# A routed expert layer behind a scan: three more tiles fixed early, twelve row places, and one weight copy on another engine

## The chip, the cores and the metric

The kernel runs on one core of a Trainium2 chip. The metric is device time in microseconds, the median of the runs shown. The trace is of one profiled execution. Its engines are TensorE (PE; PEld are its weight loads), VectorE (DVE), ScalarE (ACT), GpSimd (POOL) and SyncE (SP), each with its own instruction stream that runs in order; they meet in semaphores.

## The reference, cut to what matters

```python
x = L0_attn_x                                   # [2, 2048, 128]
mod = (_silu(c) @ wmod).reshape(2, 6, 1, -1)    # sa, ca, ga, sb, cb, gb
h = _layernorm(x) * (1 + ca) + sa
x = x + ga * linear_scan_block(h)               # gates by block-diagonal products, then a scan over the tokens
h = _layernorm(x) * (1 + cb) + sb
logits = _silu(h @ rw1 + rb1) @ rw2 + rb2       # 128 -> 512 -> 8
k_prob, k_index = softmax(top_2(logits))
for e in range(8):                              # out = sum over the two chosen experts
    we = sum(where(k_index == e, k_prob, 0))
    out += we * (_silu(h @ w1[e] + b1[e]) @ w2[e] + b2[e])   # 128 -> 512 -> 128
x = x + gb * out
```

## The kernel before, in words

The 4096 tokens are eight groups of 512. For every group the kernel normalizes (`stats1`, `norm1`), turns the rows (`turn_x`), makes the gates (`gates`, on ScalarE `tanh`, `decay`), scans, adds the residual, normalizes again and runs the router (`router`, `logits`, `sum`). VectorE chooses two experts for each token (`top2`), TensorE counts the ranks (`rank`), and `place` works out each row's place in a buffer in HBM that is sorted by expert. GpSimd sends the rows there: `send:0` to `send:15`, four indirect transfers each, 64 in all, eight for a group (L556).

The expert part works on 39 whole tiles of 256 sorted rows with one expert each. For tile s: SyncE loads the rows (L421) and TensorE transposes them (`tx`, L1234). VectorE copies them out (`xT`, L1010) and copies the expert's first and second weights (`w1`, L1019, and `w2`, L1028) after it has read the expert's number from a table into a register. TensorE runs layer 1 (`l1`, L1245), ScalarE applies silu (`hid`, L665), TensorE runs layer 2 (`l2`, L1263), ScalarE adds the bias (`yb`, L674), TensorE transposes back (`ty`, L1273), VectorE scales (`sc`, L1036), and GpSimd scatters the rows to their tokens (`scat`, two transfers of 1.0 us, L567). The transposes `tx` and `ty` share one PSUM bank, so each waits until VectorE has read the one before it.

Which tile is which expert stands in a table `tab`. `table1` (VectorE, L946 to L956) fixes the first nine tiles (`EARLY`) from the counts of the first four groups. `table1b`, `table1c` (L970 to L980) and `table2`, `table3` work out the other 30 from counts after four, six, seven and eight groups. SyncE loads tiles 0 to 8 once the sends of groups 0 to 3 have landed. The sends of groups 4 to 7 count on one semaphore, `s_disp[1]`; tiles 9 and 10 are loaded when all of it has come, and tile 10 also waits for the scatter of tile 0, because there are ten row places (`U`) in SBUF. At step 31 the hardware loop has ended, and the steps 31 to 36 also sum two expert outputs of a group into the result (`combine`, L1055 to L1057, on VectorE); step 40 and what follows sum the last groups.

The order up to tile 10 or so is written out by hand in `PLAN`, a list of steps for each engine. On VectorE the part around the tables reads

```python
norm2:7 place:4 table1:0 w1:0 top2:5 place:5 xT:0 xT:1 w2:0 table1b:0+top2:6 place:6 w1:1 table1c:0
w1:2 xT:2 xT:3 w1:3 w2:1 rowsB:0 sc:0 w2:2 top2:7 ...
```

and on TensorE

```python
... l1:0 router:31 rank:6 lev:0 tx:2 l2:0 l1:1 logits:7 tx:3 l1:2 ty:0 sum:7 l2:1 tx:4 l1:3 rank:7 ...
```

At the start TensorE's list is `warm:0 turnc:0 warm:1 mod:0 warm:2 turn_x:0 gates:0 turnb:0 turn_x:1`. `warm` are products that nobody reads. `turnb` transposes the biases (L1102) and waits for their three loads, which ScalarE orders at the start.

Of the kernel before, what the change touches and what calls it, by code (L numbers as in the profile page):

```python
# [14 lines left out]
P = 128  # L15
# [4 lines left out]
def adaln_block(nc, x, a_param, w_in, w_a, rw1, rb1, rw2, rb2, w1, b1, w2, b2, c, wmod, out):  # L20
# [25 lines left out]
    FIRST = 11  # L46
# [9 lines left out]
    LATE = TILES - EARLY  # L56
# [8 lines left out]
    with ExitStack() as ctx:  # L65
# [65 lines left out]
        yo = shared[:, 0:U * SL].rearrange("p (u n d) -> p u n d", u=U, d=D)  # L131
# [51 lines left out]
        xr = tx[:, 0:U * HALVES * ROW].rearrange("p (u n r) -> p u n r", u=U, n=HALVES)  # L183
# [29 lines left out]
        s_xnp = sem("s_xnp")  # L213
        s_root = sem("s_root")
# [16 lines left out]
        s_sc = sems(*(f"s_sc{i}" for i in range(U)))  # L231
# [22 lines left out]
        def tiles(g):  # L254
# [6 lines left out]
                warm:0 turnc:0 warm:1 mod:0 warm:2 turn_x:0 gates:0 turnb:0 turn_x:1 gates:1 turn_x:2 warm:3 turn_x:3  # L261
# [10 lines left out]
                tx:11 l1:10 ty:8 l2:9""",  # L272
# [6 lines left out]
                norm2:7 place:4 table1:0 w1:0 top2:5 place:5 xT:0 xT:1 w2:0 table1b:0+top2:6 place:6 w1:1 table1c:0  # L279
                w1:2 xT:2 xT:3 w1:3 w2:1 rowsB:0 sc:0 w2:2 top2:7 xT:4 w1:4 place:7 w2:3 sc:1 w1:5 xT:5 w2:4 table2:0  # L280
                sc:2 w1:6 xT:6 sc:3 xT:7 w2:5 w1:7 w2:6 sc:4 w2:7 xT:8 table3:0 sc:5 w1:8 w1:9 sc:6 w2:8 xT:9 w2:9
                w1:10 xT:10 sc:7 xT:11 w1:11 sc:8 w2:10""",
# [8 lines left out]
                share:5 silu:29 lgc:6 silu:30 hid:0 share:6 silu:31 hid:1 lgc:7 yb:0 hid:2 yb:1 share:7 hid:3 yb:2  # L291
                hid:4 yb:3 hid:5 yb:4 hid:6 yb:5 hid:7 yb:6 hid:8 yb:7 hid:9 yb:8 hid:10""",
# [44 lines left out]
        def levels_of(name):  # L337
            return turn_bank(name, 0)[:, 0:2 * NE]
# [25 lines left out]
        def expert_steps(eng, body, last):  # L364
            with eng.Fori(0, ROUNDS) as n:
                for u in range(U):
                    body(n * U + FIRST + u, (FIRST + u) % U)
            for s in range(FIRST + ROUNDS * U, last):
                body(s, s % U)
# [7 lines left out]
        def rounds(s, u):  # L377

            return (s - u) // U + 1

        def landed(eng, last):
            for u in range(U):
                eng.wait_ge(s_sc[u], 16 * HALVES * ((last - u) // U + 1))
# [9 lines left out]
        def _(sp):  # L393
# [22 lines left out]
            def load(s, u):  # L416
                r = sp.value_load(tab[0:1, 0, bass.ds(s, 1)], min_val=0, max_val=NE * REG)
                if not (static(s) and s < U):

                    sp.wait_ge(s_sc[u], 16 * HALVES * (rounds(s, u) - 1))  # L420
# [14 lines left out]
            for s in range(EARLY):  # L435
                if s * HALVES * ROW + HALVES * ROW > GPB * G and s * HALVES * ROW <= GPB * G:
                    sp.wait_ge(s_y, NG)
                load(s, s % U)
# [4 lines left out]
            sp.wait_ge(s_tab, 2)  # L443
            sp.wait_ge(s_pad, 16 * (NE + 1))
            sp.wait_ge(s_disp[1], 16 * TOPK * GPB * GT)
            for s in range(EARLY, FIRST):
                load(s, s % U)
# [34 lines left out]
        def _(pool):  # L482
# [67 lines left out]
            def dispatch(n):  # L550
# [27 lines left out]
        def _(act):  # L578
# [90 lines left out]

            def bias_out(s, u):  # L670
                act.wait_ge(s_l2, s + 1)
                if not (static(s) and s < 2):
# [6 lines left out]
                           "share": second_share, "hid": lambda s: hidden(s, s % U),  # L679
                           "yb": lambda s: bias_out(s, s % U)})  # L680
# [8 lines left out]
            def step(s, u):  # L689
                if static(s) and s >= TILES - 1:  # L690
                    if s == TILES - 1:
                        bias_out(s - 2, (u - 2) % U)
                        bias_out(s - 1, (u - 1) % U)
                        hidden(s, u)
                        bias_last(s, u)
                    return
                if not static(s) or s < TILES + 2:
                    bias_out(s - 2, (u - 2) % U)
                if not static(s) or s < TILES:
                    hidden(s, u)  # L700

# [6 lines left out]
        def _(dve):  # L708
# [168 lines left out]
            def place(g):  # L877
# [5 lines left out]
                dve.wait_ge(s_pos, g + 1)  # L883
                place_of = rank_bank(g).rearrange("p (j e) -> p j e", e=NE)
# [26 lines left out]
            def constants(_):  # L911
# [5 lines left out]
                v.tensor_copy(w2_s[:, :].rearrange("p (e w) -> p e w", e=NE)[:, :, HC * D:W2E], b2_c)  # L917
# [14 lines left out]
                v.memset(base[:, NENT:NENT + 1], float(4 * NE * REG))  # L932
                yield from link(v.memset(val2[:, 1, :], 1.0))
# [25 lines left out]
            def entries(_):  # L959
# [6 lines left out]
                yield from link(v.tensor_tensor(row_0[:, 0:1], row_p[:, 0:1], base[:, 0:1], ALU.add))  # L966

            def middle_levels(_):
                dve.wait_ge(s_lev, 1)
                v.tensor_tensor(cmpl[:, :, :, :], levels_of("lev").rearrange("p (l e) -> p l e", l=2).unsqueeze(3)  # L970
                                .to_broadcast([P, 2, NE, KT]),
                                kthr[:, :, 0, :].unsqueeze(1).to_broadcast([P, 2, NE, KT]), ALU.is_gt).then_inc(s_levr, 1)
                dve.wait_ge(s_levr, 1)
                yield from link(v.tensor_reduce(reach[:, :, :], cmpl[:, :, :, :], AX.X, ALU.add))
                v.tensor_tensor(nent[:, NE:2 * NE], reach[:, 0, :], full[:, :, 0], ALU.subtract)
                v.tensor_tensor(nent[:, 2 * NE:3 * NE], reach[:, 1, :], reach[:, 0, :], ALU.subtract)
                yield from link(v.scalar_tensor_tensor(base[:, 2 * NE:NENT].rearrange("p (l e) -> p l e", l=2), reach[:, :, :],
                                            float(SL), ereg[:, :].unsqueeze(1).to_broadcast([P, 2, NE]),
                                            ALU.mult, ALU.add))
                yield from link(v.tensor_tensor(dbase[:, :], base[:, 1:NENT + 1], base[:, 0:NENT], ALU.subtract))  # L980

            def late_table(_):
# [5 lines left out]
                yield from link(v.tensor_tensor(nent[:, 3 * NE:NENT], nent[:, 3 * NE:NENT], reach[:, 1, :], ALU.subtract))  # L988
# [347 lines left out]
```

## Time and profile before

| | us |
|---|---|
| median of 3 runs | 289.26 |
| lowest, highest | 288.16, 289.66 |
| the profiled execution | 288.93 |
| its span in the trace | 287.2 |
| TensorE busy | 254.2 (89%) |
| VectorE busy | 188.9 (66%) |
| GpSimd busy | 170.0 (59%) |
| ScalarE busy | 166.9 (58%) |

The profiled execution takes 1.7 us more than its span, for what lies around it. A busy share is a mean over stages with different limits; the stages have to be read one by one. The waits tell what came last at each place.

### The profile page before, as it was taken

How to read it: one execution, taken by the hardware profiler on the slowest of the kernel's cores; microseconds unless marked ns; L12 is line 12 of the kernel's file. 1: busy time of each engine (PE TensorE's matmuls, PEld its weight loads, DVE VectorE, ACT ScalarE, POOL GpSimd, SP SyncE). 2: the span in 40 equal slices, each digit the busy share in tenths (PEclk: the TensorE clock that was granted, in tenths of full speed). 3: DMA queues.
4: the chain of work that ended last, by engine and by line, in shares of the span. 5: the costliest groups of instructions: out<-in, count | busy, mean ns of one | idle time of the engine just before them, and what ended most of it. 6: DMA issues, size and time to landing. Idle time of an engine off the chain costs nothing.

```text
span 287.2 us, 4973 instructions
## 1 busy us (share of the span) xinstructions
PE 254.2 (89%) x1187; PEld 177.0 (62%) x1187; DVE 188.9 (66%) x751; ACT 166.9 (58%) x323; POOL 170.0 (59%) x192
## 2 busy tenths in 40 slices
PE   7886997998889997999998999999999999989910
PEld 3343443354244334787877888888888888867800
DVE  3959999999999987576443444444444446868333
ACT  4169999999885445544554555555555555444400
POOL 3994311267777757777777777545554545635650
PEclk9999999999999999999999999999999999999975
DMA  7994010121131226413423433222216822290504
GB/s 212 306 333 126 19 38 26 51 66 59 46 119 54 88 74 154 126 48 111 141 71 107 110 102 110 53 76 75 65 55 194 237 74 74 75 265 4 160 0 146
DMA packets 45365, 30.51 MB, mean 106 GB/s; under 512 B 5085, under 2 KB 41999, under 8 KB 45342
## 3 DMA queue, kind: packets, MB, share of 16 engines
q1 hardware_dynamic: 39888, 21.49, 27.5%
q0 software_dynamic: 4544, 8.47, 8.9%
q10 hardware_dynamic: 910, 0.30, 0.4%
q8 instruction: 8, 0.13, 0.2%
q14 instruction: 15, 0.12, 0.1%
HBM read 16.39 MB, written 12.67 MB: 101 GB/s over the span
## 4 chain that ended last, share of the span: by engine, by line
PE 43%; POOL 23%; issue 14%; DVE 12%; DMA 5%; DVEq 1%; ACT 1%; POOLq 0%; ACTq 0%; SPq 0%
POOL sorted_rows L556 21%; PE bank L1263 18%; PE bank L1245 17%; PE bank L1273 3%; PE bank L1234 2%; DVE st L722 2%; DMA expert_out<-shared,tx 2%; PE bank L1150 1%; POOL shared L520 1%; PE bank L1151 1%; PE bank L1090 1%; DVE tx L816 1%; DVE hT L821 1%; DVE shared L742 1%; DMA xs<-in_L_attn_x_dram 1%
## 5 line engine op out<-in xcount | busy, mean ns | idle before, releaser
L567 POOL DMA_INDIRECT expert_out<-shared,tx x78 | 79.3, 1016 | 54.1 <-DVE shared L1036 37.6
L665 ACT ACTIVATE hT<-bank,w_t 128x256 f32<-128x256 f32 x156 | 65.5, 471 | 29.5 <-PE bank L1245 28.6
L556 POOL DMA_INDIRECT sorted_rows<-rows,sloti x64 | 64.1, 1001 | 27.2 <-issue 18.3
L1263 PE MATMUL bank<-hT,w_t 128*128 128x256 f32 x312 | 74.1, 380 | 0.0
L1245 PE MATMUL bank<-xT,w_t 128*128 128x256 f32 x312 | 74.0, 380 | 0.0
L1245 PEld LDWEIGHTS bank<-xT,w_t 128*128 128x128 f32 x312 | 56.3, 190 | 6.6 <-DVE w_t L1019 0.5
L1263 PEld LDWEIGHTS bank<-hT,w_t 128*128 128x128 f32 x312 | 56.2, 190 | 6.3
L674 ACT ACTIVATE yT<-bank,w_t 128x256 f32<-128x256 f32 x38 | 18.0, 474 | 46.3 <-PE bank L1263 46.3
L1174 PE MATMUL bank<-h2T,rw_s 128*128 128x512 f32 x64 | 33.5, 623 | 1.0 <-ACT qv L652 0.5
L1010 DVE COPY xT<-bank 128x256 f32<-128x256 f32 x39 | 16.4, 422 | 22.4 <-PE bank L1234 22.4
L1036 DVE TENSOR_TENSOR shared<-bank,tx 128x256 f32<-128x256 f32 x38 | 16.1, 424 | 19.7 <-PE bank L1273 19.6
L1028 DVE COPY w_t<-w_s 128x513 f32 x39 | 17.8, 457 | 16.5 <-issue 15.6
L1019 DVE COPY w_t<-w_s 128x516 f32 x39 | 17.3, 443 | 16.1 <-issue 14.9
L1114 PE MATMUL bank<-ident 128*128 128x512 f32 x30 | 17.7, 702 | 2.0 <-POOL ident L492 2.0
L722 DVE BATCH_NORM_STATS2 st<-xs 128x6 f32<-128x128 f32 x64 | 15.7, 282 | 4.5 <-DMA xs<-in_L_attn_x_dram 4.4
L1174 PEld LDWEIGHTS bank<-h2T,rw_s 128*128 128x128 f32 x64 | 10.0, 189 | 12.6 <-issue 5.9
L1234 PE MATMUL bank<-ident,tx 128*128 128x128 f32 x78 | 15.2, 276 | 2.1 <-DMA tx<-sorted_rows 1.4
L1273 PE MATMUL bank<-ident,yT 128*128 128x128 f32 x76 | 14.7, 275 | 1.9 <-DVE xT L1010 1.5
L1234 PEld LDWEIGHTS bank<-ident,tx 128*128 128x128 f32 x78 | 10.4, 141 | 8.0 <-issue 2.5
L1273 PEld LDWEIGHTS bank<-ident,yT 128*128 128x128 f32 x76 | 10.1, 141 | 7.4 <-issue 4.2
L652 ACT ACTIVATE qv<-bank,smallbT 128x512 f32<-128x512 f32 x16 | 10.8, 686 | 6.4 <-PE bank L1174 6.4
L512 POOL TENSOR_TENSOR rs<-ve,half_neg 128x4 f32<-128x4 f32 x8 | 8.6, 1087 | 9.4 <-DVE ve L729 9.4
(198 smaller groups left out, 326.6 us busy)
## 6 DMA issues: line engine op xcount, KB each, us to landing
tx<-sorted_rows SPq DMA_DIRECT2D x39, 130.0 KB, 2.3
w_s<-in_L_ffn_w_dram SPq DMA_DIRECT2D x16, 256.0 KB, 6.0
xs<-in_L_attn_x_dram SPq DMA_DIRECT2D x8, 256.0 KB, 5.3
rows<-rows SPq DMA_DIRECT2D x8, 256.0 KB, 2.6
av<-expert_out SPq DMA_DIRECT2D x8, 256.0 KB, 3.7
qv<-expert_out SPq DMA_DIRECT2D x6, 256.0 KB, 5.3
expert_out<-shared,tx POOLq DMA_INDIRECT x78, 2.4
sorted_rows<-padr SPq DMA_DIRECT2D x9, 130.0 KB, 2.8
```

The source lines that it names most:

```text
L556: p.indirect_dma_start(sorted_rows[:, :], bass.IndirectOffsetOnAxis(ap=sloti[:, k, t:t + 1], axis=0), rows[:, t, k, :], None).then_inc(s_d ...
L567: p.indirect_dma_start(expert_out[:, :], bass.IndirectOffsetOnAxis(ap=xr_i[:, s % U, n, D + 1:D + 2], axis=0), yo[:, s % U, n, :], None, b ...
L665: ins = nc.scalar.activation(hsT[:, u % 2, h, :], bank[4 + q][:, (h % 2) * SL:(h % 2 + 1) * SL], ACT.Silu, bias=w1_t[:, u % 2, HID + h:HID ...
L674: nc.scalar.activation(yT[:, u % 2, :], out_bank(s)[:, 0:SL], ACT.Identity, bias=w2_t[:, u % 2, HC * D:W2E]).then_inc(s_yT_e, 1)
L722: ins = v.bn_stats(st[:, t, :], xs[:, t, :])
L1028: v.tensor_copy(w2_t[:, u % 2, :], w2_s[:, bass.ds(e * W2E, W2E)]).then_inc(s_w2t, 1)
L1114: t.matmul(bank[to][:, :].rearrange("p (k q) -> p k q", q=P), ident[:, :], ident[:, :].unsqueeze(1).to_broadcast([P, 512 // P, P]), start= ...
L1174: t.matmul(bank[2 + n % 2][:, :], rw1_s[:, h * P:(h + 1) * P], h2T[:, g % 2, :], start=True, stop=True).then_inc(s_rl1, 1)
L1234: ins = t.transpose(bank[1][:, n * P:(n + 1) * P], xr[:, u, n, 0:D], ident[:, :])
L1245: ins = t.matmul(bank[4 + h // 2][:, (h % 2) * SL:(h % 2 + 1) * SL], w1_t[:, u % 2, h * P:(h + 1) * P], xT[:, u % 2, :], start=True, stop= ...
L1263: ins = t.matmul(out_bank(s)[:, 0:SL], w2_t[:, u % 2, h * D:(h + 1) * D], hsT[:, u % 2, h, :], start=(h == 0), stop=(h == HC - 1))
L1273: ins = t.transpose(bank[1][:, n * P:(n + 1) * P], yT[:, u % 2, n * P:(n + 1) * P], ident[:, :])
```

## The change

`FIRST` goes from 11 to 12: the loops start at tile 12. A second step of the table, `tablem`, fixes tiles 9 to 11 from the counts after six groups (a product added to `rank:6`, copied out in `place:6`), `tablen` takes them off the rest, and `table1c` becomes smaller. The sends of groups 4 and 5 get their own semaphore; behind it SyncE loads tiles 9 to 11, ahead of the pads. There are twelve row places; the two new ones hold tiles 0 and 1, the other tiles go round in ten as before. The second weights are copied by ScalarE (`weights2`, right behind `hid` in the loop, ahead of it in most of the written order), no longer by VectorE. TensorE's `turnb:0` stands ahead of `warm:1`. The sums move to steps 32 to 36 and 38.

```diff
-    FIRST = 11
+    FIRST = 12
+    SLOTS = 12
+    NEXT = FIRST - EARLY
...
-                warm:0 turnc:0 warm:1 mod:0 warm:2 turn_x:0 gates:0 turnb:0 turn_x:1 gates:1 turn_x:2 warm:3 turn_x:3
+                warm:0 turnc:0 turnb:0 warm:1 mod:0 warm:2 turn_x:0 gates:0 turn_x:1 gates:1 turn_x:2 warm:3 turn_x:3
...
-                norm2:7 place:4 table1:0 w1:0 top2:5 place:5 xT:0 xT:1 w2:0 table1b:0+top2:6 place:6 w1:1 table1c:0
-                w1:2 xT:2 xT:3 w1:3 w2:1 rowsB:0 sc:0 w2:2 top2:7 xT:4 w1:4 place:7 w2:3 sc:1 w1:5 xT:5 w2:4 table2:0
+                norm2:7 place:4 table1:0 w1:0 top2:5 place:5 xT:0 xT:1 table1b:0+top2:6 place:6 w1:1 tablem:0 tablen:0
+                table1c:0 w1:2 xT:2 xT:3 w1:3 rowsB:0 sc:0 top2:7 xT:4 w1:4 place:7 sc:1 w1:5 xT:5 table2:0 sc:2 w1:6
...
-                share:5 silu:29 lgc:6 silu:30 hid:0 share:6 silu:31 hid:1 lgc:7 yb:0 hid:2 yb:1 share:7 hid:3 yb:2
+                share:5 silu:29 lgc:6 silu:30 hid:0 w2:0 share:6 silu:31 hid:1 w2:1 lgc:7 yb:0 w2:2 hid:2 yb:1 w2:3
+                share:7 hid:3 yb:2 w2:4 hid:4 yb:3 w2:5 hid:5 yb:4 w2:6 hid:6 yb:5 w2:7 hid:7 yb:6 w2:8 hid:8 yb:7
...
-        SUMS = {FIRST + ROUNDS * U: 0, FIRST + ROUNDS * U + 1: 1, FIRST + ROUNDS * U + 2: 2,
-                FIRST + ROUNDS * U + 3: 3, MID + 12: 4, FIVE + 5: 5, TILES + 1: 6}
+                FIRST + ROUNDS * U + 3: 3, FIRST + ROUNDS * U + 4: 4, TILES - 1: 5, TILES + 1: 6}
+        def slot(s):
+            return U + s if s < SLOTS - U else s % U
...
+            sp.wait_ge(s_tab, 2)
+            sp.wait_ge(s_disp[1], 16 * TOPK * GPB // 2 * GT)
+            for s in range(EARLY, FIRST):
+                load(s, slot(s))
             sp.wait_ge(s_pads, 1)
...
-                            rows[:, t, k, :], None).then_inc(s_disp[t // (GPB * GT)], 16)
+                            rows[:, t, k, :], None).then_inc(s_disp[max(0, t // GT - GPB + 2) // 2], 16)
...
+            def weights2(s, u):
+                if static(s) and s == 0:
+                    act.wait_ge(s_tab, 1)
+                if static(s) and s == EARLY:
+                    act.wait_ge(s_tab, 2)
+                e = act.value_load(tab[0:1, 1, bass.ds(s, 1)], min_val=0, max_val=NE - 1)
+                if static(s) and s == 0:
+                    act.wait_ge(s_w2, 16 * NE)
+                    act.wait_ge(s_constd, 1)
+                if not (static(s) and s < 2):
+                    act.wait_ge(s_yT_e, s - 1)
+                nc.scalar.copy(w2_t[:, u % 2, :], w2_s[:, bass.ds(e * W2E, W2E)]).then_inc(s_w2t, 1)
...
+            def middle_table(_):
+                yield from link(v.tensor_tensor(cmpk[:, :, :, :], count6[:, :].unsqueeze(2).unsqueeze(3)
+                                                .to_broadcast([P, NE, 2, KT]), kthr[:, :, :, :], ALU.is_gt))
+                v.tensor_copy(mbase[:, 0:NE], base[:, 0:NE])
+                yield from link(v.tensor_reduce(reach6[:, :, :], cmpk[:, :, :, :], AX.X, ALU.add))
+                yield from link(v.tensor_tensor(low[:, :], full[:, :, 0], reach6[:, :, 1], ALU.min))
+                v.tensor_tensor(more[:, 0:NE], low[:, :], taken[:, :], ALU.subtract)
+                v.scalar_tensor_tensor(mbase[:, NE:2 * NE], low[:, :], float(SL), ereg[:, :], ALU.mult, ALU.add)
+                yield from link(v.tensor_tensor(more[:, NE:2 * NE], reach6[:, :, 1], low[:, :], ALU.subtract))
+                v.tensor_tensor(mval[:, 0, :], mbase[0:1, 1:2 * NE + 1], mbase[0:1, 0:2 * NE], ALU.subtract)
+                yield from link(v.tensor_tensor_scan(mupto[:, :], one[:, 0:2 * NE], more[:, :], 0.0, ALU.mult, ALU.add))
+                yield from link(v.scalar_tensor_tensor(mval[:, 0, :], more[0:1, :], -float(SL), mval[:, 0, :], ALU.mult, ALU.add))
...
+                yield from link(v.tensor_reduce(tfm[:, :, :], cmpn[:, :, :, :], AX.X, ALU.add))
+                yield from link(v.tensor_scalar(tfm[:, 0, :], tfm[:, 0, :], mbase[0:1, 0:1], None, ALU.add))
+                v.tensor_tensor(tab[:, :, EARLY:FIRST], tfm[:, :, :], taus[:, :, 0:NEXT], ALU.add).then_inc(s_tab, 1)
+                dve.wait_ge(s_tab, 2)
+            def remaining(_):
+                yield from link(v.scalar_tensor_tensor(tk[:, :], mupto[:, :], -1.0, more[:, :], ALU.mult, ALU.add))
...
             def step(s, u):
...
-                if not static(s) or s < TILES:
-                    weights2(s, u)
...
+                if g == 6:
+                    t.matmul(counted_6(), ones_h[:, :], mboth[:, 6, 0, :], start=True, stop=True)
```

`link` lets VectorE wait for the end of an instruction before the next one that reads its result.

## Rows read from the trace of the kernel before

**Rows 1.** Busy us (instructions): stretch, length, PE, PEld, DVE, ACT, POOL, granted clock, DMA, GB/s.

```profile
60.00:80.00 20.00, 17.07 (x79) 7.68 (x74) 19.08 (x106) 18.43 (x28) 15.38 (x16) 1.00 0.21 65
120.36:146.29 25.93, 25.14 (x136) 20.98 (x135) 16.06 (x58) 13.40 (x32) 19.83 (x21) 1.00 0.31 94
155.80:159.69 3.89, 3.89 (x23) 3.38 (x21) 1.80 (x4) 2.13 (x5) 2.98 (x4) 1.00 0.50 133
241.48:263.67 22.19, 20.43 (x102) 16.52 (x101) 17.54 (x36) 10.77 (x26) 11.12 (x10) 1.00 0.42 122
```

**Rows 2.** Timeline, first 23 us: start, duration, engine, line, operation, count, idle before.

```profile
4.15 2.08 PE L1114 MATMUL bank<-ident 128*128 128x512 f32 x2
9.59 1.11 PE L1090 MATMUL bank<-ident,shared 128*128 128x128 f32 x4 [0.37 <-POOL shared L520]
15.34 0.33 PE L1102 MATMUL bank<-ident,smallb 44*128 44x44 f32 x1
17.59 2.08 PE L1150 MATMUL bank<-hT,wx_bd 128*128 128x512 f32 x2 [0.87 <-ACT hT L600]
19.46 1.62 PE L1151 MATMUL bank<-hT,wa_bd 128*128 128x512 f32 x2
22.23 0.69 DVE L808 SCALAR_TENSOR_TENSOR tx<-tx,hT 128x512 f32<-128x512 f32 x1 [0.44 <-ACT shared L609]
```

**Rows 3.** Timeline, the first scatter, `xT:9` and `tx:10`.

```profile
146.12 0.99 POOL L567 DMA_INDIRECT expert_out<-shared,tx  x1 [0.30 <-issue]
150.45 0.42 DVE L1010 COPY xT<-bank 128x256 f32<-128x256 f32 x1 [0.51 <-PE bank L1234]
151.62 0.44 PE L1234 MATMUL bank<-ident,tx 128*128 128x128 f32 x2 [1.21 <-DMA tx<-sorted_rows]
```

**Rows 4.** DMA queue of ScalarE's loads, 6.5 to 7.0 us: packets, MB, share.

```profile
q10 hardware_dynamic: 5, 0.00, 1.2%
```

**Rows 5.** Timeline, VectorE: linked steps of `rstd2`, and of `table1`.

```profile
99.04 0.16 DVE L795 TENSOR_TENSOR root_t<-root 128x4 f32<-128x4 f32 x1
99.24 0.16 DVE L796 TENSOR_TENSOR root_t<-root_t,half_v 128x4 f32<-128x4 f32 x1
...
103.39 0.41 DVE L946 TENSOR_TENSOR cmpk<-bank,kthr 128x256 f32<-128x256 f32 x1
...
105.70 0.17 DVE L956 TENSOR_TENSOR tab<-tf,taus 1x18 int32<-1x18 f32 x1
```

**Rows 6.** Timeline, 115 to 120 us: from `place:6` to `tx:3`.

```profile
115.08 0.17 DVE L880 TENSOR_SCALAR rows<-tdl 128x4 f32<-128x4 f32 x1 [0.32 <-ACT tdl L657]
...
116.97 0.42 DVE L970 TENSOR_TENSOR cmpl<-bank,kthr 128x256 f32<-128x256 f32 x1
...
119.03 1.06 PE L1181 MATMUL bank<-qv,rw_s 128*32 128x512 f32 x8
119.55 0.42 DVE L1010 COPY xT<-bank 128x256 f32<-128x256 f32 x1
120.11 0.41 PE L1234 MATMUL bank<-ident,tx 128*128 128x128 f32 x2
```

**Rows 7.** Groups by line, whole span: busy us, mean ns of one, idle before.

```profile
L1028 DVE COPY w_t<-w_s 128x513 f32 x39 | 17.8, 457 | 16.5 <-issue 15.6 <-ACT yT L674 0.9
L634 ACT COPY h2T<-bank 128x512 f32<-128x512 f32 x8 | 4.7, 586 | 3.9 <-PE bank L1090 3.8
```

**Rows 8.** Busy time by stretch around gaps of TensorE; columns as in rows 1.

```profile
26.00:28.40 2.40, 0.21 (x2) 0.01 (x1) 2.33 (x7) 2.38 (x5) 1.87 (x3) 1.00 0.00 0
107.50:109.50 2.00, 0.23 (x7) 0.17 (x6) 1.83 (x18) 1.36 (x3) 1.66 (x2) 1.00 0.52 126
276.50:277.00 0.50, 0.00 (x0) 0.00 (x0) 0.50 (x1) 0.00 (x0) 0.29 (x1) 0.66 0.00 0
```

**Rows 9.** Timeline: the last matmuls, and one pass of a sum.

```profile
249.88 0.69 DVE L1056 TENSOR_TENSOR qv<-qv,gbB 128x512 f32<-128x512 f32 x1
...
274.03 0.59 PE L1289 MATMUL bank<-ident,yT 128*128 128x128 f32 x2 [0.46 <-ACT yT L686]
```

More of the change, by code:

```diff
@@ L224, in adaln_block @@
             "s_dlt", "s_tdl", "s_slot", "s_cnt", "s_tab", "s_pads", "s_pad")
-        s_disp = sems("s_disp0", "s_disp1")
-        s_xr = sems(*(f"s_xr{i}" for i in range(U)))
+        s_disp = sems("s_disp0", "s_disp1", "s_disp2")
+        s_xr = sems(*(f"s_xr{i}" for i in range(SLOTS)))
         s_txp, s_xT, s_w1t, s_w2t, s_l1, s_hs, s_l2, s_yT_e, s_yturn, s_yo, s_fin = sems(
@@ L230, in adaln_block @@
         s_out = sem("s_out")
-        s_sc = sems(*(f"s_sc{i}" for i in range(U)))
+        s_sc = sems(*(f"s_sc{i}" for i in range(SLOTS)))
         s_y01 = sems(*(f"s_y01_{g}" for g in range(NG)))
@@ L240, in rank_bank, with counted_6 @@
             return bank[7][:, 0:GT * NE] if g < GPB else bank[6][:, GT * NE:2 * GT * NE]
+        def counted_6():
+            return bank[6][:, 2 * GT * NE + NE:2 * GT * NE + 2 * NE]
         def counted():
@@ L377, in rounds, with step_slot @@
         def rounds(s, u):
-            return (s - u) // U + 1
+            if static(s) and s < SLOTS:
+                return 1
+            return (s - u) // U + 1 if u >= SLOTS - U else (s - u - U) // U + 1
+        def step_slot(s, u, by):
+            return slot(s + by) if static(s) else (u + by) % U
+        def slot(s):
+            return U + s if s < SLOTS - U else s % U
         def landed(eng, last):
-            for u in range(U):
-                eng.wait_ge(s_sc[u], 16 * HALVES * ((last - u) // U + 1))
+            for u in range(SLOTS):
+                eng.wait_ge(s_sc[u], 16 * HALVES * len([s for s in range(last + 1) if slot(s) == u]))
         def load_last(eng, k):
@@ L417, in load @@
                 r = sp.value_load(tab[0:1, 0, bass.ds(s, 1)], min_val=0, max_val=NE * REG)
-                if not (static(s) and s < U):
+                if not (static(s) and s < SLOTS):
                     sp.wait_ge(s_sc[u], 16 * HALVES * (rounds(s, u) - 1))
@@ L442, in _ @@
                 padding(bass.ds(sp.value_load(pad_i[0:1, e:e + 1], min_val=e * REG, max_val=e * REG + TOK), SL))
-            sp.wait_ge(s_tab, 2)
+            sp.wait_ge(s_tab, 3)
             sp.wait_ge(s_pad, 16 * (NE + 1))
-            sp.wait_ge(s_disp[1], 16 * TOPK * GPB * GT)
-            for s in range(EARLY, FIRST):
-                load(s, s % U)
+            sp.wait_ge(s_disp[2], 16 * TOPK * GPB // 2 * GT)
             def load_and_y(s, u):
@@ L973, in middle_levels @@
                 dve.wait_ge(s_levr, 1)
[L974 to L979, printed above, removed]
+                v.scalar_tensor_tensor(base[:, 2 * NE:3 * NE], reach6[:, :, 0], float(SL), ereg[:, :], ALU.mult, ALU.add)
@@ L1220, in count_levels @@
                 wait_turn_bank(pe, "lev", 0)
-                t.matmul(levels_of("lev").rearrange("p (l e) -> p l e", l=2), ones_h[:, :], mboth[:, 6:8, 0, :],
-                         start=True, stop=True).then_inc(s_lev, 1)
+                t.matmul(counted_7(), ones_h[:, :], mboth[:, 7, 0, :], start=True, stop=True).then_inc(s_lev, 1)
             def turn_table(_):
```

124 lines of the change are left out of this document (74 added, 50 removed).

## The prediction

> **What bounds the kernel now.** I read the stretches of the span first, then the chain of waits, then the timeline of the places where one stage hands over to the next. Three limits follow one another. Up to about 107 us VectorE is full (19.08 of 20 us) [rows 1], behind a start in which TensorE, still at its slower rate, decides when the gate products arrive [rows 2]. From 58 to 144 us GpSimd sends rows out in 64 transfers, and TensorE already works on whole tiles beside it. From about 152 us on TensorE alone decides: one tile takes 3.89 us, in which TensorE is never idle, VectorE works 1.80 us and ScalarE 2.13. In the last steps, which also sum into the output, VectorE decides: five tiles take 22.19 us in place of 19.45 [rows 1].
>
> The point to see is the hand-over. Tile 10 is loaded behind all sends and behind the scatter of tile 0, and TensorE stands idle for 1.21 us [rows 3]. This is what the change goes for. But the chain of waits names only what came last; TensorE also needs tile 9 copied out of the shared bank before it may transpose tile 10. Tile 9's copy ends at 150.87, so without the load tile 10's transposes would start there and not at 151.62 [rows 3]. **The load costs 0.7 us, not 1.21.**
>
> **The change, part by part, against the profiled execution's 288.93 us.**
>
> *Start.* `turnb:0` is moved ahead of `warm:1`. It waits for three small loads of the biases; their queue still moved 5 packets between 6.5 and 7.0 us [rows 4], so TensorE waits until about 7.0. Queued behind it are `warm:1`, `mod:0`, `warm:2` and `turn_x:0`. The first three took from 4.15 to 9.22 (9.59 less 0.37 idle), 5.1 us [rows 2], so `turn_x:0` starts near 12.1 in place of 9.59: 2.5 us late. `turnb` itself no longer stands at 15.34, so some 2.2 us remain at `gates:1` (17.59). How much arrives depends on TensorE's rate: two products of 512 columns took 2.08 us at 17.59, the pair begun at 19.46 only 1.62 [rows 2], so the rate doubled near 20.5. If it does so at the same time again, `gates:1` runs mostly at the fast rate and ends about 1.1 us late; if earlier, 0.4; if later, 2.5. VectorE, which had waited 0.44 us for this product at 22.23 [rows 2], is full from there to 107 us, so what arrives stays. It also gets two memsets more in `consts` (0.1 us). I take **+1.0**, ends +0.3 and +2.6.
>
> *Tables.* Before, VectorE did only the middle levels between `w1:1` and `w1:2`, from 116.97 on, and `xT:2` was done at 119.97 [rows 6]. The change puts `tablem` and `tablen` there. `tablem` has 15 instructions. Two run over 256 elements, 0.41 us and a step of 0.45; nine small ones are waited for before the next starts, in steps of 0.20 (L795 to L796) [rows 5] to 0.25, one of them wider, which I take at 0.33; four follow at 0.08. That is 0.90 + 8 x 0.23 + 0.33 + 0.32 = 3.4 us. For comparison, the first table with its 8 instructions took from 103.39 to 105.87, 2.5 us [rows 5]. `tablen` has eight, five of them linked: 5 x 0.21 + 3 x 0.08 = 1.3 us. In `table1c` two passes over 256 elements (0.42 us) [rows 6] become half as long: -0.3. Net +4.4 us. Ahead of that, `w2:0` now stands on ScalarE between `hid:0` and `share:6`. `place:6` had waited 0.32 us for `share:6` at 115.08 [rows 6], so a copy of 0.7 us ahead of it plus the new copy of the sixth group's counts (0.25) makes `w1:1` some 1.05 us late. **`xT:2` ends 5.5 us later.** Nothing hides this: `tx:3` may not write the shared bank before `xT:2` has read it, and every later tile is queued behind `tx:3`. TensorE went from `logits:7` (119.03 to 120.09) straight into `tx:3` (120.11) [rows 6]; now it idles about 4.5 us between them.
>
> It gets some back. In the 25.93 us from `l1:2` to `l1:8` TensorE works 25.14 [rows 1]; the other 0.8 goes, since VectorE no longer copies `w2` (0.46 us each) [rows 7] after reading a tile number for it. The 0.7 us at tile 10 goes as well. Tile 12 is then the first behind all sends, on `scat:2`, two scatters later than tile 10 was; at 1.0 + 0.3 us a transfer [rows 3] that is 5.2 us after 151.6, near 157 plus the start's delay, and TensorE, late by then, asks for it near 162: no wait. 5.5 - 0.8 - 0.7 gives **+4.0** at `l1:9`; with the linked steps at 0.17 to 0.25 us and ScalarE's copy at 0.5 to 1.0, the ends are +2.9 and +4.8.
>
> *TensorE's clock.* A gap of 4.5 us is new. Before, gaps of 2.2 us (26.2 to 28.4) and 1.8 us (107.55 to 109.33) left the granted clock at 1.00. But after the last matmul, which ends at 274.6 [rows 9], it fell within 276.5 to 277.0: mean 0.66 [rows 8]. So I expect it to fall inside the gap to the lower of its two levels, 1.2 GHz. How long it stays there is not shown; from 17.59 on TensorE worked some 3 us before its rate doubled [rows 2]. I take 3.6 us of work at the low rate, which loses half: **+1.8**, ends 0 and +3.5.
>
> *`w2` on ScalarE.* The copy of 513 columns isn't there; the nearest rows are ScalarE's copy of 512 from PSUM, 0.59 us, and VectorE's own of 513, 0.46 [rows 7]. I take 0.7, since ScalarE's silu of 256 costs 0.47 and most of its 512 rows on the page lie at 0.6 to 0.72, and keep 0.5 to 1.0. In the loop ScalarE is idle 1.76 of 3.89 us [rows 1], and `ty` asks for `yb` some 1.6 us after `yb` can start: nothing, until a copy takes about 1.7 us. The notes speak against this move: the Trainium skill, "ScalarE: Activation LUTs", section on rules for kernel authors, says to use VectorE rather than ScalarE for plain arithmetic, and budgets about 0.3 us and 0.83 ns an element. By it a copy takes 0.73 us, an estimate near the rows. The rule prices the instruction, not the queue it stands in, and the sum stays.
>
> *Last steps.* VectorE's step with a sum is xT, w1, sc, w2 and three passes of 0.69 us [rows 9]; five such tiles take 22.19 us, 2.7 over TensorE's 19.45 [rows 1]. Without `w2`, and starting each instruction as the one before drains, VectorE needs 0.33 + 0.43 + 0.42 + 2.06, 3.3 us, under TensorE's 3.89. The sums move one step later, the fifth to step 38, beside work with room. **-2.7**, ends -3.2 and -1.5.
>
> *Free of cost:* the split `lev` count, the count product in `rank:6` (0.1 us), the two row places, the load of tiles 9 to 11 (ordered some 16 transfers of 1.3 us ahead of the last send's end, near 127, and wanted near 154), and the pads, sent later but long before tile 12. Without their covers each costs under 1 us.
>
> Sum: +1.0 + 4.0 + 1.8 - 2.7 = **+4.1**, 293.0 us; the median of the runs shown is 0.33 above the profiled one, so 293.3.
>
> **The rivals.**
> 1. *TensorE is late, its clock stays up*, because what it does just before and behind the gap is enough to hold it. For it: 2.2 us did no harm. Against: 4.5 is twice that. 291.5. The Trainium skill, "TensorE: Matmul & The Clock Gate", Part 1, says the engine is at 1.2 GHz after an idle stretch and needs sustained work to get back. The fall at the end of this trace agrees; no run here shows what a gap in the middle does.
> 2. *Faster: the tables cost VectorE little.* The place is `xT:2`. If the linked instructions overlap so that it ends only 2 us later, the 1.5 us of stalls given back nearly cover it, the clock stays, and the sums decide: +1.0 + 0.5 - 2.7 gives 288.1; with no delay at all 286.1. It turns at a delay of 3.2 us. Against: linked steps at 0.20 us and more.
> 3. *Start absorbed, small delay in the middle, clock up*: 0.3 + 2.9 - 2.7 gives 289.8, no change.
> 4. *ScalarE becomes the bound*, if its read of the tile number can't run ahead. Above 1.7 us a copy it decides; 0.3 us over on 30 steps gives 302.
> 5. *The clock comes back late, in the start and after the gap*: 2.6 + 4.0 + 3.5 - 2.7 gives 296.7.
>
> **How the numbers follow.** Forecast 0.42, rival 1 0.20, rival 2 0.11, rival 3 0.15, rival 4 0.04, rival 5 0.08. A measurement of this kernel can't tell changes within 0.5%, 1.45 us, from none (287.8 to 290.7). Faster: rival 2 and a little of rival 3, 0.13. Same: most of rival 3 and the low side of rival 1, 0.17. Slower: 0.70. The range leaves out rivals 2 and 4 and reaches to 3 and 5: 289.5 to 297.
>
> **What the profile after should show.** `turnb` near 7.0 us and `turn_x:0` near 12.1. Between the `w1` copies of tiles 1 and 2 some 7 us instead of 2.6, and TensorE idle ahead of `tx:3` for 4 to 5 us, released by VectorE's `xT`. A granted clock under 1.00 right there. No wait for a load at tiles 9 to 12. Steps of 3.89 us from tile 9 to 37, sums and all. ScalarE's new copy at 0.7 us. I am wrong if the gap at `tx:3` is under 3 us, if the start's delay is gone at 22 us, or if the steps with sums still take 4.2.

## The result and the profile after

| | before | after |
|---|---|---|
| median (six runs each) | 289.00 us | 293.48 us |
| ratio, 95% interval | | 1.0141 [1.0081, 1.0200] |
| profiled execution, its span | 288.93, 287.2 | 293.04, 291.3 |
| VectorE busy | 188.9 | 175.9 |
| ScalarE busy | 166.9 | 186.8 |
| TensorE busy | 254.2 | 253.8 |

One of the six runs of after took 906 us; without it their median is 293.17. A run more than 1.5% above the fastest of its kernel counts as slow and is left out of the ratios, though not of the medians: here the 906 us, below three of the four runs of `turnb_back` and single ones of `warm_gap`, `turnb_back_3` and `after_again`. The change makes the kernel slower by 1.4%. Below, "marker" is the start of a named step in the trace.

The stretches, after, with the columns of [rows 1]: tiles 2 to 8 (one microsecond longer than from `l1:2` to `l1:8`), one step of the loop, the six steps 31 to 36, of which five hold a sum, and the place where the clock was low.

```profile
129.15:155.10 25.95, 25.95 (x140) 22.46 (x140) 13.51 (x52) 16.04 (x39) 19.86 (x21) 0.99 0.38 109
162.90:166.80 3.90, 3.90 (x23) 3.39 (x22) 1.28 (x3) 2.63 (x7) 2.98 (x4) 1.00 0.43 119
244.69:268.06 23.37, 23.37 (x122) 20.31 (x121) 16.25 (x32) 16.18 (x37) 13.30 (x12) 1.00 0.44 127
126.26:129.80 3.54, 2.94 (x12) 1.20 (x13) 1.85 (x8) 1.53 (x3) 2.84 (x3) 0.52 0.17 56
```

TensorE is busy in every microsecond of the first three. In the third, six steps take 23.37 us, 3.895 each, with VectorE at 16.25: the sums no longer set the pace. This is what the change gains. Now what it pays, first the start (timeline of after; columns as in [rows 2]).

```profile
7.80 0.30 PE L1167 MATMUL bank<-ident,smallb 44*128 44x44 f32 x1 [3.57 <-DMA smallb<-in_L_ffn_b_dram]
...
12.88 1.06 PE L1155 MATMUL bank<-ident,shared 128*128 128x128 f32 x4
...
20.50 2.07 PE L1215 MATMUL bank<-hT,wx_bd 128*128 128x512 f32 x2 [0.99 <-ACT hT L629]
...
22.37 1.85 PE L1216 MATMUL bank<-hT,wa_bd 128*128 128x512 f32 x2
...
25.37 0.69 DVE L852 SCALAR_TENSOR_TENSOR tx<-tx,hT 128x512 f32<-128x512 f32 x1 [3.68 <-ACT shared L638]
```

`turnb` waits 3.57 us for the biases, `turn_x:0` begins 3.29 us later than in [rows 2], and TensorE is still at its slow rate at 22.37. VectorE's second group (`input:1`) begins at 25.37 in place of 22.23. Then the tables (same view).

```profile
119.35 1.99 PE L1329 MATMUL bank<-hT,w_t 128*128 128x256 f32 x8 [0.36 <-ACT w_t L710]
119.51 0.17 DVE L924 TENSOR_SCALAR rows<-tdl 128x4 f32<-128x4 f32 x1 [1.44 <-ACT tdl L686]
...
120.86 0.43 DVE L1095 COPY w_t<-w_s 128x516 f32 x1 [0.53 <-issue]
121.24 0.42 DVE L1017 TENSOR_TENSOR cmpk<-count,kthr 128x256 f32<-128x256 f32 x1
...
124.34 0.15 DVE L1034 TENSOR_TENSOR tab<-tfm,taus 1x6 int32<-1x6 f32 x1
...
125.63 0.16 DVE L1045 TENSOR_TENSOR nent<-nent,tk 128x8 f32<-128x8 f32 x1
125.83 0.29 DVE L1049 TENSOR_TENSOR cmpl<-bank,kthr 128x128 f32<-128x128 f32 x1
...
126.26 1.84 PE L1246 MATMUL bank<-qv,rw_s 128*32 128x512 f32 x8 [2.93 <-DVE cmpl L1049]
...
127.79 0.43 DVE L1095 COPY w_t<-w_s 128x516 f32 x1 [0.78 <-DVE dbase L1056]
128.14 0.42 DVE L1086 COPY xT<-bank 128x256 f32<-128x256 f32 x1
...
128.70 0.66 PE L1300 MATMUL bank<-ident,tx 128*128 128x128 f32 x2 [0.60 <-DVE xT L1086]
```

From `w1:1` (120.86) to `w1:2` (127.79) 6.9 us pass. `xT:2` starts at 128.14 and had started at 119.55 [rows 6]: 8.59 later. TensorE's idle time stands ahead of `logits:7` (L1246): that product writes a bank which `table1c` reads last at L1049, and behind the new tables this read comes late. The copy that moved to ScalarE (groups by line):

```profile
L710 ACT COPY w_t<-w_s 128x513 f32 x39 | 24.2, 620 | 2.2 <-ACT yT L716 1.8
```

The account of the profiled execution, marker against marker:

| stretch | before | after | difference |
|---|---|---|---|
| to the first table (last instruction) | 105.70 | 108.98 | +3.28 |
| first table to `xT:2` | 13.85 | 19.16 | +5.31 |
| `xT:2` to `l1:2` | 0.81 | 1.01 | +0.20 |
| `l1:2` to `l1:8` | 25.93 | 24.94 | -0.99 |
| `l1:8` to `l1:9` | 5.61 | 4.91 | -0.70 |
| `l1:9` to `l1:37` | 111.77 | 109.06 | -2.71 |
| `l1:37` to the last matmul | 10.36 | 10.09 | -0.27 |
| sum | | | +4.12 |

### The profile page after: what moved, and what is told of

It is laid out like the page before. It is cut to its first block, busy times and chain, and to the rows that moved or that the text cites. A ratio compares the mean times of both kernels' runs of the same rounds, so it can differ in the third digit from the quotient of the medians.

```text
span 291.3 us, 5027 instructions
## 1 busy us (share of the span) xinstructions
PE 253.8 (87%) x1188; PEld 178.7 (61%) x1188; DVE 175.9 (60%) x738; ACT 186.8 (64%) x363; POOL 169.8 (58%) x192
## 4 chain that ended last, share of the span: by engine, by line
PE 55%; DVE 30%; DMA 4%; issue 4%; ACT 2%; POOL 1%; ACTq 1%; SPq 1%; POOLq 0%; DVEq 0%
PE bank L1311 22%; PE bank L1329 22%; PE bank L1300 3%; DVE rows L884 3%; DVE rows L891 3%; PE bank L1339 3%; DVE st L766 3%; DVE hT L865 2%; DVE xs L871 2%; PE bank L1179 2%; DVE tx L860 2%; DMA smallb<-in_L_ffn_b_dram 2%; POOL expert_out L596 1%; PE bank L1215 1%; DVE shared L786 1%
## 5 line engine op out<-in xcount | busy, mean ns | idle before, releaser
L710 ACT COPY w_t<-w_s 128x513 f32 x39 | 24.2, 620 | 2.2 <-ACT yT L716 1.8
L541 POOL TENSOR_TENSOR rs<-ve,half_neg 128x4 f32<-128x4 f32 x8 | 8.7, 1089 | 12.8 <-DVE ve L773 12.8
L577 POOL TENSOR_TENSOR rs<-ve,half_neg 128x4 f32<-128x4 f32 x4 | 4.1, 1037 | 15.7 <-DVE ve L773 15.7
```

Source lines behind the costliest of these rows:

```text
L710: nc.scalar.copy(w2_t[:, u % 2, :], w2_s[:, bass.ds(e * W2E, W2E)]).then_inc(s_w2t, 1)
```

## Experiments

"Before" in what follows is the kernel before, run on the same chip beside the others: 289.17 us for the first four runs, 289.44 for the next four, 289.54 for `turnb_back_3`. The ratio is to that. My theory is the prediction's sum. The main rivals are that the start, or the clock, or ScalarE carries the 4 us.

### The start alone: `turnb:0` early in the kernel before

```diff
-warm:0 turnc:0 warm:1 mod:0 warm:2 turn_x:0 gates:0 turnb:0 turn_x:1
+warm:0 turnc:0 turnb:0 warm:1 mod:0 warm:2 turn_x:0 gates:0 turn_x:1
```

> The kernel before with turnb:0 ahead of warm:1 and nothing else. Theory: +3.2 us, 292.3, with turn_x:0 near 12.9, input:1 near 25.4 and all later stages shifted alike. Rival, the forecast's value: +1.0, 290.1, because the rate of TensorE doubles at the same time as before.

Measured 290.81 us (10 runs), ratio 1.0046 [1.0001, 1.0091]: +1.3 us by the ratio (1.6 by the medians), the rival's side. In its trace `turn_x:0` begins at 12.69, as late as in after, but TensorE's rate doubles earlier (the pair at 20.30 took 1.12 us, not 2.07), and `input:1` begins at 23.44, 1.2 us later than in the kernel before, where the rate doubled at about the same time (20.5). So the rival's condition held, and with it its price. In after the rate doubled later, near 24, and all 3.3 us arrived: the delay's price depends on when the rate doubles.

### `turnb:0` back in its place, in the changed kernel

The diff above, reversed, on the changed kernel.

> The changed kernel with one thing undone: turnb:0 stands behind gates:0 again. Theory: TensorE's wait for the bias loads at the start (3.6 us) arrives whole at the end, since TensorE and then VectorE decide up to the tables; turn_x:0 starts at 9.6 again, the first table ends near 105.9, and the kernel takes 290.2 us (3.2 less than the changed one, ratio to before 1.004). Rival: GpSimd's sends or the tables absorb the start, as the forecast's lower end had it; then it stays above 292.5.

Measured 293.57 us, four runs: 293.45, 293.89, 293.68, and one of 288.97. The theory had 290.2, and the four runs lie on both sides of it; they settle nothing (`turnb_back_3` below has twelve). The profiled execution is the one of 293.45. In it `turn_x:0` begins at 9.47, `input:1` at 21.54 and the first table ends as early as in before (105.69), so the start is repaired. But the clock fell three times behind it, near 29, 111 and 128 us. The stretch between two short gaps, and layer 1 of tile 0 in it (windows, then timeline, of `turnb_back`):

```profile
110.50:117.50 7.00, 6.55 (x20) 5.22 (x20) 2.50 (x23) 1.99 (x5) 5.30 (x6) 0.52 0.73 168
```
```profile
109.33 0.19 PE L1272 MATMUL bank<-mboth,before 128*128 128x32 f16 x1 [1.79 <-DVE mboth L916]
...
113.24 3.76 PE L1311 MATMUL bank<-xT,w_t 128*128 128x256 f32 x8
```

The granted clock is 0.52 for 7 us behind an idle time of 1.79 us. The same gap is in the kernel before and cost nothing there [rows 8]. Eight products take 3.76 us, not 1.99. In this execution the clock gave back what the start had won. No other trace from a chip without pauses has this stretch, so it explains the one execution, not the kernel.

> The changed kernel with turnb:0 back behind gates:0, on a chip on which the kernel before is hoped to take its usual 289. The delay of turn_x:0 costs 1.3 us on average, as alone in the kernel before: 292.2. Or the early start is given back by TensorE's clock in the middle: 293.5, and the trace shows the granted clock fallen ahead of 120 us again. Without such a stretch in this trace, input:1 should start near 22.0 us, the first table near 105.7 and xT:2 near 125.0.

On another chip: 290.84 us (12 runs), ratio 1.0052 [1.0022, 1.0083], against 1.0141 for the change whole. The trace has no low stretch at 110 us. Its first table ends at 105.31 and `xT:2` starts at 124.70, where 125.0 was expected. Between first table and `xT:2` stand 19.4 us, as in after: **the tables' price does not depend on the start**. The median lies 1.4 under the 292.2 of the first theory, so the delay here cost some 2.6 us (0.89% of 289; the two intervals allow 0.6 to 4.5), and 1.3 in the kernel before (0 to 2.6). What can be said is some 1 to 3 us.

### `w2` on ScalarE alone, in the kernel before

```diff
-                if not static(s) or s < TILES:
-                    weights2(s, u)
...
+            def weights2(s, u):
+                e = act.value_load(tab[0:1, 1, bass.ds(s, 1)], min_val=0, max_val=NE - 1)
...
+                nc.scalar.copy(w2_t[:, u % 2, :], w2_s[:, bass.ds(e * W2E, W2E)]).then_inc(s_w2t, 1)
```

> The kernel before with only the copies of w2 moved to ScalarE. Theory: the steps with sums fall to 3.89 us (-2.7 to -3.0), the hand-over at tile 10 stays bound by the load, so 286.3. Rival: VectorE's relief is worth little because w2's copy was hidden, and share:6 behind w2:0 costs 0.6: 289.5.

Measured 285.52 us, ratio 0.9833 [0.9735, 0.9931]: faster than both kernels. Its windows (tiles 2 to 8, and six steps with sums in their old places):

```profile
121.14:145.77 24.63, 24.63 (x137) 21.10 (x135) 13.46 (x51) 16.37 (x39) 18.54 (x21) 1.00 0.32 96
237.11:260.48 23.37, 23.37 (x122) 20.31 (x121) 18.43 (x35) 16.10 (x37) 13.66 (x12) 1.00 0.43 127
```

TensorE idles in neither. The first took 25.93 us before and the second's six steps are 3.895 each. All of the change's gain but the 0.7 us at tile 10 is in this one part, and the sums need not have been moved. The rival's price for `w2:0` ahead of `share:6` is there too, but small beside it: from the first table to `xT:2` it takes 14.71 us, 0.86 more than before.

### The tables behind `xT:2`

```diff
-xT:0 xT:1 table1b:0+top2:6 place:6 w1:1 tablem:0 tablen:0 table1c:0 w1:2 xT:2 xT:3 w1:3 rowsB:0 sc:0 top2:7
+xT:0 xT:1 table1b:0+top2:6 place:6 w1:1 levc:0 w1:2 xT:2 tablem:0 xT:3 w1:3 tablen:0 sc:0 table1c:0 top2:7
```

`levc` is the first instruction of `table1c`, the read for which `logits:7` waits.

> The changed kernel with VectorE's order changed: the read of the shared bank for the seventh group's count (levc) and w1:2, xT:2 come before tablem; tablen follows w1:3, table1c follows sc:0, and rowsB goes behind sc:7. Theory: the gap ahead of logits:7 and tx:3 goes and the granted clock stays at 1.00; the steps 0 to 8 are then held by VectorE a little (0.5 to 1 us), so it saves 3.5 to 4.5 us: 289.3. Rival: VectorE's table work is merely late elsewhere (rank:7, ty:0) and TensorE loses as much there: 292 or more.

Measured 288.05 us (10 runs), ratio 0.9942 [0.9900, 0.9984], 5.4 us under after, where the theory had 3.5 to 4.5; in the profiled executions 2.3 us of the difference lie in the start, which is the same code in both. VectorE around `xT:2` (timeline: `w1:1`, `levc`, `w1:2`, `xT:2`, the first and the last instruction of `tablem`):

```profile
118.36 0.43 DVE L1097 COPY w_t<-w_s 128x516 f32 x1 [0.72 <-issue]
118.75 0.29 DVE L1049 TENSOR_TENSOR cmpl<-bank,kthr 128x128 f32<-128x128 f32 x1
119.61 0.43 DVE L1097 COPY w_t<-w_s 128x516 f32 x1 [0.58 <-issue]
119.96 0.42 DVE L1088 COPY xT<-bank 128x256 f32<-128x256 f32 x1
120.29 0.41 DVE L1017 TENSOR_TENSOR cmpk<-count,kthr 128x256 f32<-128x256 f32 x1
...
123.41 0.15 DVE L1034 TENSOR_TENSOR tab<-tfm,taus 1x6 int32<-1x6 f32 x1
```

From the first table to `xT:2` it takes 13.27 us, not 19.16, and the granted clock stays at 1.00. The tables themselves are all still there, and they are not free at the later place: from the first table to `l1:8` pass 41.11 us, 0.96 more than in `w2_alone` (40.15), which has neither of the new tables. In after it is 45.11. **The change is slow mainly because of where its tables stand.** In after, from `w1:1` to `w1:2` they hold VectorE for 6.9 us while `tx:3` waits for `xT:2` behind them, and nothing needs their result so early: with `tablem` done at 123.56, tile 10 costs no more wait (4.99 us from `l1:8` to `l1:9`, against 5.61 before).

> The changed kernel with the tables spread as in the run tables_later, turnb:0 back behind gates:0, and w2:0 behind share:6 on ScalarE. If the terms add (start -3.2, tables -4.0, share -0.5), 285.6 us, 1.2% under before. Rival: with the start's delay gone, tile 12 has to wait for the sends and scat:2, and 1 us or more of it comes back: 287.

Measured 285.21 us, ratio 0.9875 [0.9788, 0.9962], four runs, as the theory had it. With `share:6` back ahead of `w2:0` the first table to `xT:2` is 12.35 us: 0.9 less; the prediction gave 0.7 of its 1.05 us to that order. It beats both kernels too, but not `w2_alone` by anything that can be measured. Three more tiles chosen early gave nothing beyond the copy's move: the 0.7 us won at tile 10 is about what the tables still cost (0.96).

### TensorE kept at work in the gap

```diff
-l2:0 l1:1 logits:7 tx:3 l1:2
+l2:0 l1:1 warm:10 logits:7 tx:3 l1:2
```

`warm:10` is four products of 512 columns that nobody reads; the trace records each as two instructions, eight in 3.60 us.

> The changed kernel with four instructions of 512 columns that nobody reads in TensorE's gap ahead of logits:7. Theory: the granted clock stays at 1.00, logits:7 takes 1.06 us again and not 1.84, but its end lies under VectorE's table work, so only 0.3 to 0.6 us are saved: 292.9. Rival, the forecast's value: the low clock costs 1.8 us, so 291.6.

Measured 291.22 us (10 runs), ratio 1.0055 [1.0010, 1.0099]; the trace, seven microseconds around the gap, and the same for `turnb_back_3`, which has the gap but not the filler (windows):

```profile
122.00:129.00 7.00, 6.07 (x31) 3.25 (x29) 4.89 (x23) 3.36 (x8) 5.37 (x6) 1.00 0.23 68
```
```profile
122.00:128.50 6.50, 5.18 (x17) 2.94 (x18) 4.28 (x15) 2.52 (x5) 4.95 (x6) 0.51 0.31 81
```

With the filler the clock stays at 1.00, and the kernel is 2.3 us faster than after though it does more: the expectation's rival (291.6), not its theory (292.9), and what rival 1 of the prediction described (291.5) brought about by hand. Not all of the 2.3 need be the clock's. The intervals of the two ratios allow 0.3 to 4.6 us, and between the two profiled executions 2.1 us lie in the start, which is the same code, and 0.5 behind the gap. What speaks for the clock beyond these two is that the mean granted clock of the ten runs is 0.976 to 0.983 and of the five of after 0.964 to 0.975. The traces of the kernels with the gap say how its price varies: from `l1:2` to `l1:8` it takes 24.60 us with the clock up, and 24.94 in after, 25.89 in `turnb_back`, 26.19 in `turnb_back_3`, 26.81 in `act_512` and 28.77 in `act_1536`, where the low stretch was 10 us long (3.4 in after). The extra is 0.3 to 4.2 us, with 1.6 in the middle.

### How much ScalarE has left

```diff
             def weights2(s, u):
...
+                if not static(s):
+                    nc.scalar.copy(hT[:, TOK // 2:TOK // 2 + 512], w2_s[:, 0:512])
                 nc.scalar.copy(w2_t[:, u % 2, :], w2_s[:, bass.ds(e * W2E, W2E)]).then_inc(s_w2t, 1)
```

> The changed kernel with a second copy on ScalarE in each of the 20 looped steps, 512 columns into a part of SBUF that nobody reads (0.62 us). ScalarE's step becomes 2.17 + 0.62 + 0.62 = 3.4 us of 3.89. Theory: it still fits, no change (293.4, within 0.5). Rival: ScalarE was already close to deciding, each step grows by 0.3 and more: 299.

> The same with 1536 columns (1.5 us). ScalarE's step becomes 4.3 us and decides: at least 0.4 us on each of 20 steps, 301 to 304. If it stays under 296, ScalarE's work overlaps in a way that the busy sum doesn't tell.

The second kernel copies 1536 columns in place of 512. Measured 293.79 us, ratio 1.0153 [1.0052, 1.0253], and 294.74 us, ratio 1.0186 [1.0101, 1.0270]. The first is near what was expected, though its two runs lie 3.3 us apart (292.15 and 295.42). The second is a miss: 301 or more was expected, with the remark that a time under 296 would mean overlap. Loop steps with 1536 columns (windows of 39 us; timeline of ScalarE):

```profile
180.00:219.00 39.00, 39.00 (x202) 33.92 (x201) 12.78 (x30) 38.74 (x71) 19.70 (x21) 1.00 0.24 65
```
```profile
204.54 0.63 ACT L712 COPY w_t<-w_s 128x513 f32 x1
205.06 0.48 ACT L718 ACTIVATE yT<-bank,w_t 128x256 f32<-128x256 f32 x1
205.48 1.70 ACT L694 ACTIVATE hT<-bank,w_t 128x256 f32<-128x256 f32 x4
207.07 1.47 ACT L711 COPY hT<-w_s 128x1536 f32<-128x1536 f32 x1
208.43 0.63 ACT L712 COPY w_t<-w_s 128x513 f32 x1
```

ScalarE is busy 38.74 of 39.00 us and TensorE all 39.00. The durations of a step add up to 4.28 us, but each instruction starts some 0.1 us before the one ahead ends (205.06 less 204.54 is 0.52, for a duration of 0.63), so from copy to copy pass 3.89 us: just the step. From `l1:9` to `l1:31` both kernels and after take 85.7 us. The second kernel's 1 us more in the median is not in the loop (the two intervals overlap, and each has two runs); its trace has it in the longer low stretch ahead of `l1:8`.

### Three kernels on a chip that paused

> The changed kernel itself once more, beside the next two, because its traces and those of its variants differ in where TensorE's granted clock first rises (13 to 24 us) and in how often it falls between 108 and 134 us. Expected 293.5, from 292.5 to 294.5. Its own trace should again show the clock fallen in the gap ahead of tx:3; whether the stretch at the low level is 3.4 us long as before or longer, and whether input:1 starts at 25 us or nearer 22, is open.

> The changed kernel with turnb:0 back behind gates:0, once more with more runs (293.6 in few runs, though turn_x:0 began 3.4 us earlier). Three theories. The delay costs here what it cost in the kernel before, 1.3 us: 292.2. The delay costs all that the markers of the first two traces showed at 22 us, 3.3: 290.2. Or the earlier start is given back in the middle, where its first trace shows VectorE ahead of TensorE and TensorE's clock low from about 110 to 116 us: 293.5. The last one predicts such a stretch in this trace too; without it the first one should hold.

> The changed kernel with turnb:0 back behind gates:0 and four products of 512 columns that nobody reads in the gap ahead of logits:7. If the two repairs are independent: 293.5 less 2.3 (what the unread products alone gave) less 1.3 = 289.9. If the gap's clock costs nothing, and 2.3 was only the scatter of the executions, 292.2. If the start costs nothing in the changed kernel, 291.2.

On this chip the kernel before took 329.73 us (29 runs), and these 328.45, 328.21 and 328.90 (12 each): ratios 0.9971 [0.9932, 1.0010], 0.9941 [0.9910, 0.9972] and 0.9985 [0.9949, 1.0020]. None of the expectations can be read against that. The waits of VectorE and ScalarE from 78 to 195 us in `after_again` (line, waited for: us in all, times, longest):

```profile
DVE best L902 <- remote: 11.5, 2, 7.3
DVE xT L1086 <- remote: 10.9, 3, 6.3
DVE shared L1103 <- remote: 8.1, 1, 8.1
```
```profile
ACT hT L694 <- remote: 19.9, 3, 10.7
```

Engines stand idle up to 10.7 us at a time, and the trace names nothing of this core as their releaser. This is so only from about 77 to 190 us; from `l1:9` to `l1:37` the kernel takes 109.06 us, as elsewhere, and the busy time of VectorE and ScalarE is that of after (176.2 and 186.8 us), so their instructions are no longer than there. What paused them stays open. One thing can be used. Ahead of the pauses, `turn_x:0` at 12.76 and `input:1` at 21.72 stand beside 9.58 and 22.07 of `turnb_back_2`: 3.2 us of delay had vanished by 22 us, since in the second the granted clock was at 0.50 from about 12 to 22 us. Again the rate, not the delay, decides.

## Why the prediction was right, point by point

The time (293.3 against 293.48) and its direction were right. The terms, each against its measurement:

*The bounds and what is gained: right.* -2.7 for the sums (measured -2.71), -0.8 for the stalls (-0.99, and without the low clock's part some -1.3, as in `warm_gap`), -0.7 for the load of tile 10 (-0.70). The chain of waits had 1.21 us on that load [rows 3], and reading on to the copy of tile 9 gave the true size.

*The tables: right.* +5.5 was worked out from the linked steps of [rows 5], 5.31 measured, and `tables_later` shows it is their place. The parts: `tablem` 3.25 us (121.24 to 124.49), predicted 3.4; `tablen` 1.3 (124.53 to 125.79), predicted 1.3; the delay ahead of `w1:1` 0.96 (from the first table 10.92 us before, 11.88 in after), predicted 1.05, though its two terms, 0.7 and 0.25, add up to 0.95. Most of it is the order of `w2:0` and `share:6`: 0.86 in `w2_alone`.

*What was wrong in this part.* TensorE's idle time was expected ahead of `tx:3`, 4 to 5 us long. It was 2.93 us ahead of `logits:7` and 0.60 ahead of `tx:3`. The step that failed is the sentence that TensorE "went from `logits:7` straight into `tx:3`" [rows 6] and would idle between them; that `logits:7` itself writes a bank that `table1c` has to read was overlooked. It cost the time nothing, as `tx:3` waits for VectorE anyway. But it means that the clock fell behind an idle time of 2.9 us, not of 4.5: rival 1's case against itself, that 4.5 is twice the harmless 2.2, was not put to the test. By the prediction's own words, a gap under 3 us at `tx:3` should have shown it wrong; the marker was badly chosen, `xT:2` was the right one.

*The start: mis-sized in the profiled execution, right on average.* The term was +1.0 with ends at +0.3 and +2.6; the profiled execution has +3.28, outside. `turnb` ran at 7.80 and not 7.0: the last packets of its load in [rows 4] are not yet the moment its semaphore lets TensorE go. And the rate doubled after 24 us there, against 20.5 before. Over executions it is less: 1.3 us by `turnb_alone`; the first tables of the six traces with an early `turnb` end at 106.57 to 108.98, middle 106.9, those of the five with the old place at 105.31 to 106.52, middle 105.7 (the paused chip left out).

*The clock: mis-sized the other way, right on average.* The term was +1.8 with ends 0 and +3.5. The profiled execution paid 0.5 (0.20 ahead of `l1:2`, 0.3 in the 24.94 us behind it), since most of the low time fell under the tables, where VectorE decided. By `warm_gap` against after it is up to 2.3 in the median, by the other traces 1.3 to 4.2. So in the one execution the errors cancelled: start +2.3, clock -1.3, stalls -0.5, tables -0.2, the end -0.3, in all 0.0. The 4.1 of that trace is partly luck. In the medians the two terms hold, within wide intervals. Each got one number with ends, and the upper end of the start's (+2.6) was too low: it counted the delay that is left at `gates:1`, but not that the rate may double later than in the trace of before, which costs even a kernel without the delay.

The Trainium skill, "TensorE: Matmul & The Clock Gate", Part 1, says that the engine drops to 1.2 GHz after an idle stretch. The gap near 124 us (2.87 to 2.93 us long) agrees in all five traces that have it, and `warm_gap`, where it is filled, stays at 1.00. After the shorter gaps of 2.2 and 1.8 us it happened in some traces and not in others (last section).

*ScalarE: right that it costs nothing, the point from which it decides was too low.* The copy took 0.62 us, 0.7 was taken. ScalarE decides not from 1.7 us but from about 1.9: the 0.52 us step of the copy and the 1.36 us of the 1536-column one fit in, with next to nothing left (1.9 us in all). The read of the tile number did not hold it up. Rival 4 needed three times the copy that there is.

By the Trainium skill, "ScalarE: Activation LUTs", section on rules for kernel authors, the copy would take 0.73 us, an estimate from its budget for an instruction with its bias as a pointer operand. It took 0.62. The section's advice to use VectorE for plain arithmetic does not carry over to this copy, since in the steps with sums VectorE was the fuller engine (17.54 us of 22.19, ScalarE 10.77 [rows 1]): the copy's move gained 3.7 us.

## What to carry to other kernels

An addition to an in-order engine costs what it delays at its place, not what it contains: the same tables delay the next copy by 4.3 us when they stand ahead of it and TensorE waits for it, and cost about 1 us behind it. Take a change of several parts apart: the one part that carried the gain (one copy on the emptier engine, -3.7 us) was alone as fast as anything in the study. And where TensorE goes idle for a few microseconds, price its clock as a distribution, and look at more than one execution before believing a term of a sum.

## What the runs showed of the hardware

- *A gap of the same length does or does not lower the clock.* Some 1.8 us of idle time at 107.5 us left it at 1.00 in the kernel before [rows 8] and was followed by 7 us at 0.52 in `turnb_back`. The gap of 2.2 us that begins at 26.2 us in the kernel before, and which the prediction took for harmless, left the clock at 1.00 in seven of the eleven traces without pauses; in `turnb_back`, `best1`, `act_512` and `act_1536` (gaps of 2.2 to 2.3 us) it fell right behind it, for 3.4 us. That costs 0.55 us: from `input:1` to the next group's `input:2` pass 13.3 us in these four and 12.7 in the others. Timeline and windows of `best1`:

```profile
28.11 0.78 PE L1157 MATMUL bank<-ident,hT 128*128 128x128 f32 x4 [2.33 <-DVE hT L865]
28.68 1.92 PE L1217 MATMUL bank<-hT,wx_bd 128*128 128x512 f32 x2
```
```profile
28.50:32.00 3.50, 3.50 (x7) 1.53 (x6) 3.46 (x10) 2.54 (x4) 1.29 (x9) 0.51 0.13 38
```

  The low stretches behind the gap near 124 us were 3.4 to 10 us long in five traces of kernels that have it.
- *At the start TensorE's rate is not what the granted clock says.* In after the pair of 512-column products begun at 14.90 took 2.05 us and the one at 20.50 still 2.07, while the granted clock read 1.00. In `act_512`, with the same code up to there, the pair at 15.07 took 1.10. Windows of after, timeline of `act_512`:

```profile
14.00:20.00 6.00, 4.61 (x8) 2.06 (x8) 5.58 (x39) 2.06 (x4) 5.90 (x8) 1.00 1.12 331
```
```profile
15.07 1.10 PE L1217 MATMUL bank<-hT,wx_bd 128*128 128x512 f32 x2 [0.96 <-ACT hT L629]
```

  The slow rate of the start ended somewhere between 14 and 24 us of the span, in no order that the code explains. In `turnb_back_3` it had ended once already, near 6 us, and come back at 9.5; from that fall on the granted clock reads 0.50, until 16.3. The slow stretch from the start of a trace up to the first rise reads 1.00 in all of them. What moves the rise stays open. It is why a delay of 3.3 us costs anything from nothing to all of it.
- *ScalarE's recorded durations overlap* by about 0.1 us an instruction: 4.28 us of them fit in a step of 3.89.
- *On one chip engines stood idle* for up to 10.7 us at a time with no releaser in the trace, in one part of the kernel only, and the change of 1.4% was not to be seen there (ratio 0.9971).
